# Expert products with the weights held in TensorE, and the routing weight applied at the last eviction

## What is computed

```python
router_probs = softmax(x @ gate_weight.T)              # 32 experts
router_top_value, router_indices = top_k(router_probs, 8)
...                                                    # 4 primary choices; a secondary one is moved
...                                                    # to the most similar primary if that is >= 0.5
combine = sum(one_hot(rerouted_indices) * routing_weights)     # tokens x 32
def expert_step(y, params):
    wgu, wd, cw = params                               # 384x512, 512x192, one weight per token
    g, u = split(x @ wgu.T, 2, axis=-1)
    h = silu(g) * u
    return y + h @ wd.T * cw[:, None], None
```

## Time and profile before

| | |
|---|---|
| median of 3 runs | 1722.84 us (1722.58 to 1733.0) |
| the profiled execution | 1730.1 us, of which the span from the first to the last instruction is 1728.3 us |
| mean granted TensorE clock | 0.941 of 2.4 GHz |
| busy share of the span | PE 86%, DVE 57%, ACT 41%, POOL 43% |
| PE matmuls | 11445 in the whole program |
| DMA | 269.44 MB, mean 156 GB/s |
| chain that ended last | PE 63%, DVE 15%, DMA 10%, issue 5%, ACT 4%, POOL 3% |

### The profile page before, as it was taken

One profiled execution on the slowest core, in us unless ns is written; L12 is line 12 of the kernel. 1 busy time (PEld: TensorE's weight loads), 2 busy tenths in 40 slices (PEclk: granted clock), 3 DMA queues, 4 the chain that ended last, 5 costly groups with the idle time before them and its releaser, 6 DMA issues.

```text
span 1728.3 us, 33963 instructions
## 1 busy us (share of the span) xinstructions
PE 1481.2 (86%) x11445; PEld 837.2 (48%) x11446; DVE 989.4 (57%) x1922; ACT 715.4 (41%) x1291; POOL 748.5 (43%) x671
## 2 busy tenths in 40 slices
PE   1199999986999999999998458988988999999980
PEld 0166666652444444445554314655555566565650
DVE  5767777766675757553489793433333344344437
ACT  4233433335546464643464342433333344444440
POOL 0134444443001010134345625565566766666654
PEclk9699999997999999999999568999999999999995
DMA  8211111115877676751011126999999977777868
GB/s 331 83 29 24 24 35 26 24 25 190 311 242 260 227 260 227 261 196 48 17 38 51 51 98 181 236 270 246 255 272 243 196 142 146 138 146 142 144 107 298
DMA packets 95640, 269.44 MB, mean 156 GB/s; under 512 B 15104, under 2 KB 15520, under 8 KB 90848
## 3 DMA queue, kind: packets, MB, share of 16 engines
q1 hardware_dynamic: 59968, 182.75, 31.2%
q0 software_dynamic: 35616, 85.99, 25.2%
HBM read 158.84 MB, written 101.47 MB: 151 GB/s over the span
## 4 chain that ended last, share of the span: by engine, by line
PE 63%; DVE 15%; DMA 10%; issue 5%; ACT 4%; POOL 3%; SPq 0%; DVEq 0%; ACTq 0%; POOLq 0%
PE bank L490 14%; PE bank L796 14%; PE bank L817 8%; DMA acc<-X,WA 8%; PE bank L613 6%; PE bank L619 6%; PE bank L636 6%; PE bank L787 3%; DVE ARENA L985 2%; ACT ARENA L1270 2%; PE bank L806 1%; DMA ARENA<-acc 1%; DVE ARENA L1158 1%; PE bank L717 1%; DVE bs L859 1%
## 5 line engine op out<-in xcount | busy, mean ns | idle before, releaser
L796 PE MATMUL bank<-ARENA,XT 128*128 x1908 | 368.1, 330 | 1.8 <-DVE XT L1232 1.8
L1631 POOL DMA_INDIRECT acc<-X,WA x159 | 252.7, 1589 | 185.3 <-ACT X L1270 152.4
L796 PEld LDWEIGHTS bank<-ARENA,XT 128*128 128x128 f16 x1908 | 182.0, 99 | 126.0 <-issue 11.1
L817 PE MATMUL bank<-ARENA,XT 128*128 x795 | 200.1, 383 | 26.9 <-issue 18.8
L1232 DVE COPY XT<-bank 128x1024 f16<-128x1024 f16 x159 | 109.8, 690 | 191.3 <-PE bank L787 138.0
L1270 ACT ACTIVATE ARENA<-ARENA 128x512 f16<-128x512 f32 (+1 forms) x128 | 92.7, 735 | 265.9 <-DVE ARENA L1018 131.3
L490 PE MATMUL bank<-WA,XT 128*128 128x512 f16 (+1 forms) x768 | 140.0, 337 | 69.7 <-DVE ARENA L926 34.6
L1625 POOL DMA_INDIRECT XT<-x_rows,WA x159 | 156.9, 987 | 56.8 <-issue 35.3
L1508 POOL TENSOR_TENSOR rstd<-mv,mhalf 128x1 f32<-128x1 f32 x44 | 18.9, 430 | 311.0 <-DVE mv L862 311.0
L490 PE MATMUL bank<-XT,STG 128*128 128x512 f16 x640 | 148.6, 379 | 0.0
L1242 DVE SCALAR_TENSOR_TENSOR XT<-bank,XT 128x192 f32<-128x192 f32 x159 | 66.4, 418 | 136.0 <-ACT XT L1485 114.5
(11 more groups left out here) (214 smaller groups left out, 2376.0 us busy)
## 6 DMA issues: line engine op xcount, KB each, us to landing
WA<-w_exp SPq DMA_DIRECT2D x64, 640.0 KB, 5.2
w_scratch<-WA SPq DMA_DIRECT2D x64, 640.0 KB, 3.9
ARENA<-w_scratch SPq DMA_DIRECT2D x32, 1280.0 KB
ARENA<-ARENA SPq DMA_DIRECT2D x64, 128.0 KB, 2.3
acc<-ARENA SPq DMA_DIRECT2D x18, 256.0 KB, 3.0
x_rows<-ARENA SPq DMA_DIRECT2D x17, 256.0 KB, 2.0
STG<-xT SPq DMA_DIRECT2D x8, 512.0 KB, 5.9
X<-x SPq DMA_DIRECT2D x1, 4096.0 KB, 16.3
```

The costliest lines, as they stand in the source:

```text
L796: mm = pe.matmul(d, xTb[k.u % 2][:, a * KD + kd, :], weights(sl, b, kd * 2 * DFF, 2 * DFF), start=(a, b, kd) == (0, 0, 0), stop=(a, b, kd) ...
L817: mm = pe.matmul(d, hT[k.u % 2][:, c, :], weights(sl, j, c0, DIM), start=n == 0, stop=n == 4)
L1631: pool.indirect_dma_start(acc[i % 2], bass.IndirectOffsetOnAxis(blkidx[:, i:i + 1], 0), yD[i % 4], None, compute_op=ALU.add).then_inc(y_ou ...
```

## The change

- `gate_up` holds the weights and moves the tokens. For each of three groups `c` of 128 features it makes 12 matmuls of 128 moving columns, each with its own held 128x128 of weights: 36 matmuls in place of 12. The result has features on partitions, and the host lays the 384 rows of the weights out in a new order: gate 0 to 127, then up 128 to 191 with gate 128 to 191, then up 0 to 127.
- With features on partitions h needs no transposing: `h_transposes`, `ht_evac` and `hB` go. ACT takes the SiLU in two instructions, DVE multiplies 256 columns, ACT writes the high half straight into `hT`, and DVE the low half.
- The routing weight can't be applied there any more, as tokens are now along the columns. It is the scale of `y_evac`, read from `xg` through a register, so ACT runs `load_packs` in place of DVE, and the factor 1/256 goes into the router's product (L1121).
- `expert_down` runs two blocks behind, between the first and the second group of `gate_up`. Its fifth matmul contracts over 64 rows alone, in place of the third block of `hT`.
- `gather` waits until the result of the block that used the buffer is evicted (`y_sb`).

```diff
-            def gate_up(k, sl, some):
-                d = bank[2 + k.u % 2][:, 0:2 * DFF]
-                for a, b, kd in some:
-                    mm = pe.matmul(d, xTb[k.u % 2][:, a * KD + kd, :], weights(sl, b, kd * 2 * DFF, 2 * DFF),
-                                   start=(a, b, kd) == (0, 0, 0), stop=(a, b, kd) == (1, 0, KD - 1))
+            def gate_up(k, sl, c):
+                d = bank[2 + k.u % 2][:, c * P:(c + 1) * P]
+                n = 0
+                for a, b in ((0, 0), (0, 1), (1, 0)):
+                    for kd in range(KD):
+                        mm = pe.matmul(d, weights(sl, b, kd * 2 * DFF + c * P, P), xTb[k.u % 2][:, a * KD + kd, :],
+                                       start=n == 0, stop=n == 3 * KD - 1)
+                        n += 1
                 return mm
...
-            def h_transposes(k):
...
             def expert_down(k, sl):
-                pe.wait_ge(ht_sb, k.i + 1)
+                pe.wait_ge(h_lo, k.i + 1)
                 if not k.before(2):
                     pe.wait_ge(y_sb, k.i - 1)
...
-                order = ((1, 0, base), (1, 1, base), (0, 0, base), (2, 0, base + DIM), (2, 1, base + DIM))
-                for n, (c, j, c0) in enumerate(order):
-                    mm = pe.matmul(d, hT[k.u % 2][:, c, :], weights(sl, j, c0, DIM), start=n == 0, stop=n == 4)
-                mm.then_inc(blk_done, 1)
+                pe.matmul(d, h[:, 1, :], w(0, base), start=True, stop=False)
+                pe.matmul(d, h[:, 1, :], w(1, base), start=False, stop=False)
+                pe.matmul(d, h[:, 2, :], w(0, base), start=False, stop=False)
+                pe.matmul(d, h[:, 0, :], w(0, base + DIM), start=False, stop=False)
+                pe.matmul(d, h[0:64, 0, :], w(1, base + DIM)[0:64, :], start=False, stop=True).then_inc(blk_done, 1)
...
-                if not k.before(3):
-                    expert_down(k.at(-3), expert_of(held["packs"], k.u - 3) % NSLOT)
                 sl = e % NSLOT
...
-                gate_up(k, sl, products[:8])
+                gate_up(k, sl, 0)
+                if not k.before(2):
+                    expert_down(k.at(-2), expert_of(held["packs"], k.u - 2) % NSLOT)
                 if not last:
                     gather_transposes(k.at(1))
-                gate_up(k, sl, products[8:]).then_inc(gu_ready, 1)
-                if not k.before(1):
-                    h_transposes(k.at(-1))
+                gate_up(k, sl, 1)
+                gate_up(k, sl, 2).then_inc(gu_ready, 1)
...

-                dve.scalar_tensor_tensor(h, bank[2 + k.u % 2][:, DFF:2 * DFF], cw, sgD[k.u % 2], ALU.mult, ALU.mult).then_inc(h_ready, 1)
+                if not k.before(2):
+                    dve.wait_ge(h_hi, k.i - 1)
+                dve.tensor_tensor(h.rearrange("p a n -> p (a n)"), bank[2 + k.u % 2][:, P:3 * P], sgD[k.u % 2].rearrange("p a n -> p (a n)"),
+                                  ALU.mult).then_inc(h_ready, 1)
                 dve.wait_ge(h_hi, k.i + 1)
-                dve.tensor_tensor(split[:, 0:P], h[:, 0:P], split[:, P:2 * P], ALU.subtract)
-                dve.tensor_tensor(split[:, 2 * P + 64:3 * P], h[:, P:DFF], split[:, 2 * P:2 * P + 64], ALU.subtract).then_inc(h_lo, 1)
+                dve.tensor_tensor(split[64:P, 0, :], h[0:64, 0, :], split[0:64, 0, :], ALU.subtract)
+                dve.tensor_tensor(split[:, 2, :], h[:, 1, :], split[:, 1, :], ALU.subtract).then_inc(h_lo, 1)
...

-                copy(yD[k.u % 4], bank[6 + k.u % 2][:, :], 1 / (WS * WS)).then_inc(y_sb, 1)
+                cw = xg[k.u % NG].bitcast(F32)[:, DIM:XROW][:, bass.ds(e, 1)]
+                act.activation(yD[k.u % 4], bank[6 + k.u % 2][:, :], ACT.Identity, scale=cw).then_inc(y_sb, 1)
...
-                act.activation(sgD[k.u % 2], bank[2 + k.u % 2][:, 0:DFF], ACT.Silu, scale=1 / WS).then_inc(sg_ready, 1)
-                if not k.before(1):
-                    ht_evac(k.at(-1))
+                act.activation(sg[0:64, 0, :], gu[64:P, P:2 * P], ACT.Silu, scale=1 / WS)
+                act.activation(sg[:, 1, :], gu[:, 0:P], ACT.Silu, scale=1 / WS).then_inc(sg_ready, 1)
...

             def gather(i):
                 if i >= NG:
-                    pool.wait_ge(h_ready, i - NG + 1)
+                    pool.wait_ge(y_sb, i - NG + 1)
```

More of the change, by code:

```diff
@@ L230, in build @@
         xTb = [r.take([2 * KD, P], F16) for _ in range(2)]
-        sgD = [r.take([DFF], F32) for _ in range(2)]
-        h32 = [r.take([DFF], F32) for _ in range(2)]
-        hB = [r.take([3 * P], F16) for _ in range(2)]
+        sgD = [r.take([2, P], F32) for _ in range(2)]
+        h32 = [r.take([2, P], F32) for _ in range(2)]
         hT = [r.take([3, P], F16) for _ in range(2)]
@@ L791, in weights, with expert_down @@
                 return Wslot[:, bass.ds(sl * (2 * WCOLS) + (j * WCOLS + c0), n)]
-            def gate_up(k, sl, some):
-                d = bank[2 + k.u % 2][:, 0:2 * DFF]
-                for a, b, kd in some:
-                    mm = pe.matmul(d, xTb[k.u % 2][:, a * KD + kd, :], weights(sl, b, kd * 2 * DFF, 2 * DFF),
-                                   start=(a, b, kd) == (0, 0, 0), stop=(a, b, kd) == (1, 0, KD - 1))
+            def gate_up(k, sl, c):
[6 more added lines that the diff above has]
+                        n += 1
                 return mm
-            def h_transposes(k):
+            def expert_down(k, sl):
                 pe.wait_ge(h_lo, k.i + 1)
[L802 to L809, removed]
-                pe.wait_ge(ht_sb, k.i + 1)
                 if not k.before(2):
@@ L814, in expert_down @@
                 base = KD * 2 * DFF
-                order = ((1, 0, base), (1, 1, base), (0, 0, base), (2, 0, base + DIM), (2, 1, base + DIM))
-                for n, (c, j, c0) in enumerate(order):
-                    mm = pe.matmul(d, hT[k.u % 2][:, c, :], weights(sl, j, c0, DIM), start=n == 0, stop=n == 4)
-                mm.then_inc(blk_done, 1)
-            products = [(a, b, kd) for a, b in ((0, 0), (0, 1), (1, 0)) for kd in range(KD)]
+                h = hT[k.u % 2]
+                w = lambda j, c0: weights(sl, j, c0, DIM)
+                pe.matmul(d, h[:, 1, :], w(0, base), start=True, stop=False)
[3 more added lines that the diff above has]
+                pe.matmul(d, h[0:64, 0, :], w(1, base + DIM)[0:64, :], start=False, stop=True).then_inc(blk_done, 1)
             held = {}
@@ L843, in _ @@
             every_block(pe, 8, expert_block, 8)
[L844 to L848, removed]
+            for j in (2, 1):
+                expert_down(Blk(0, NBLK - j, 8), expert_of(held["packs"], NBLK % 8 - j) % NSLOT)
         @block.vector
@@ L1223, in _ @@
             dve.scalar_tensor_tensor(blkidx, vzero, float(TOK), bank[5][:, 0:NBLK], ALU.add, ALU.add).then_inc(tables_ready, 1)
-            mine = {}
+            for u in range(2):
+                own.did(dve.memset(sgD[u][64:P, 0, :], 0.0))
+            own.settle()
             def xt_evac(k):
@@ L1467, in _, with y_evac @@
             row_hots(3, 0, ROWS_B)
[L1469 to L1475, removed]
+            theirs = {}
+            def y_evac(k, e):
                 act.wait_ge(blk_done, k.i + 2)
@@ L1478, in y_evac @@
                     act.wait_ge(y_out[k.u % 4], k.use(4) * 16)
-                copy(yD[k.u % 4], bank[6 + k.u % 2][:, :], 1 / (WS * WS)).then_inc(y_sb, 1)
+                cw = xg[k.u % NG].bitcast(F32)[:, DIM:XROW][:, bass.ds(e, 1)]
+                act.activation(yD[k.u % 4], bank[6 + k.u % 2][:, :], ACT.Identity, scale=cw).then_inc(y_sb, 1)
             def expert_block(k, fresh, last=False):
+                if fresh:
+                    theirs["packs"] = load_packs(act.engine, k)
                 act.wait_ge(gu_ready, k.i + 1)
@@ L1484, in expert_block @@
                     act.wait_ge(h_ready, k.i - 1)
[L1485 to L1487 removed]
+                sg, gu = sgD[k.u % 2], bank[2 + k.u % 2]
+                act.activation(sg[0:64, 0, :], gu[64:P, P:2 * P], ACT.Silu, scale=1 / WS)
+                act.activation(sg[:, 1, :], gu[:, 0:P], ACT.Silu, scale=1 / WS).then_inc(sg_ready, 1)
                 act.wait_ge(h_ready, k.i + 1)
                 if not k.before(2):
[L1490 to L1491 removed]
+                    act.wait_ge(blk_done, k.i)
+                copy(hT[k.u % 2][:, 0:2, :].rearrange("p a n -> p (a n)"), h32[k.u % 2].rearrange("p a n -> p (a n)")).then_inc(h_hi, 1)
                 if not k.before(2):
[L1493 to L1498 removed]
+                    y_evac(k.at(-2), expert_of(theirs["packs"], k.u - 2))
+            every_block(act, 8, expert_block, 8)
+            for j in (2, 1):
+                y_evac(Blk(0, NBLK - j, 8), expert_of(theirs["packs"], NBLK % 8 - j))
         @block.gpsimd
@@ L1666, in _layouts @@
     }
-    gu = i["L1_ffn_gate_up_proj"].transpose(0, 2, 1).reshape(EXPERTS, KD, P, 2 * DFF).transpose(0, 2, 1, 3)
+    feats = np.r_[0:P, DFF + P:2 * DFF, P:DFF, DFF:DFF + P]
```

(1 more changed line is left out.)

23 lines of the change are left out of this document (7 added, 16 removed).

## The result

The changed kernel takes 1846.9 us (median of 4 runs, 1845.8 to 1848.3), the kernel before in the same comparison 1727.3 (1722.6 to 1733.0): 119.6 us more, ratio 1.069, 95% interval 1.065 to 1.074. The profiled execution took 1846.4 us; its span is 1842.9 us against 1728.3, 114.6 more. The forecast was 1835 in a range of 1795 to 1900.

A forecast was written before the change was run, and what follows sets the result against it. PE's array mostly bounds the expert stage before; after, its sequencer's address work does: 2.4 + 2.1 - 0.1 + 0.28, unrounded 4.64 us, over 159 blocks, 738 for 627, +111 on 1722.8, said as 1835 us, range 1795 to 1900.

The forecast's parts named there:

- The address steps: PE's sequencer in gate_up: 24 weight addresses per block in place of 8, 16 more at 0.13 us, +2.1 us.
- the rival's 1710: Forecast time if PE's array, not its sequencer, set the pace at 3.53 us per block; chance 0.11.
- The sum of a block: PE's sequencer, expert stage: 2.4 base + 2.1 addresses - 0.1 dropped wait + 0.28 reload, 4.64 us per block.
- The even 4.6 us named as a sign: Expected sign in the expert stage: L1485, run once per block, would come at an even 4.6 us.
- the range's lower end: Expert stage: 1795 us, tied to 4.4 us per block; an address step of 0.10 us gave 4.2.
- The array's time: PE's matmuls and transposes per block: 3.65 + 0.05 for products - 0.17 for h's transposes, 3.53 us.
- Down products: 0: expert_down on PE: still five products of 512 columns, contracting over 64 rows changes nothing, 0 us.
- What was put at 0: ACT, DVE, POOL's gather and scatter, the router's product and the DMA-bound stretch: hidden or unchanged, 0 us.
- The router's product: L1121, four runs at 1.23 us: its form with a scalar costs 0 to +5 us, taken as 0.
- The array stays the bound: Rival, PE in the expert stage: sequencer total under 3.65 us, array 3.53 per block, 1710 us; chance 0.11.
- The load of the held operand shows: Rival, PE's products: weight loads of 0.098 us unhidden, 5.2 us per block, +200, 1923 us; chance 0.04.
- More than I count: Rival, PE: third pass recomputes addresses (2080 us), granted clock falls, or instruction fetches (from +36); chance 0.10 together.

The follow-up runs named there:

- e1: Kernel before, operands as they were, its products cut into 36 matmuls of 128 moving columns with 24 weight addresses per block; 1871.1 us, ratio 1.083.
- e2: As e1, but all three groups read the first group's weights, so 8 addresses per block; 1746.8 us, ratio 1.012.
- e12: As e10, but with each address worked out one by one, as in the change; 1832.6 us, ratio 1.061.
- e10: As e9, with TensorE's reload of the expert numbers moved behind the down products of each eighth block; 1713.2 us, ratio 0.990.
- e5: As e4, with the addresses of each group of matmuls worked out ahead of it in packed register instructions; 1772.3 us, ratio 1.026.
- e6: As e5, with the fifth down product over 128 rows in place of 64; 1763.5 us, ratio 1.019.
- e9: As e6, with the gathered block's transposes ahead of the down products and their evacuation ahead of DVE's subtractions; 1734.8 us, ratio 1.003.
- e7: Changed kernel with only the fifth down product over 128 rows in place of 64; 1846.3 us.
- e4: Changed kernel with slots read through a view of bytes, so each address is one operation and not a packed three; 1782.2 us, ratio 1.032.
- e3: Changed kernel with all three groups reading the first group's weights, so 8 addresses per block; 1786.9 us, ratio 1.034.
- e11: Kernel before with only TensorE's reload of the expert numbers moved, behind the first eight products of each eighth block; 1734.8 us, ratio 1.003.

## Why the prediction was right

**The bound.** The forecast was that the array would wait for addresses. e1 and e2, and e12 and e10, differ in the address work and in nothing else, with 124.2 and 119.4 us between them. The whole loss of 119.6 is of that size. It isn't the only layer: packing alone gives back 74.6 (e5), the other 45 lie under it and come out only with e6 (8.9), e9 (28.7) and a part of the reload's move.

**The address steps.** 24 a block, forecast and counted without exception. The 0.13 us a step, read from trains behind a reload, holds in a steady block too (7 gaps in 0.9 to 1.0 us, 15 in 2.0). The 46 ns of the rows was the trap: by it the sequencer would have fitted under the array, and the forecast would have been the rival's 1710.

**The sum of a block.** 2.4 + 2.1 - 0.1 = 4.4 us (4.36 unrounded) was forecast for a block without reload; the 118 such blocks of the loop take 4.31 on average. The reload was put at 2.2 us, 0.28 a block; it costs 2.3 in its own block and 0.2 in the one behind, 0.30 a block. What the sum put at nothing is the clock. The block behind a reload takes 4.5 us where the clock stayed at 1.00 and 5.4 where it fell to 0.50, and that is 12 x 0.87 = 10 us, 0.07 a block. Together they make 4.68, as measured (744 us over 159 blocks), where 4.64 was forecast. So the miss of some 6 us is small partly by luck: 0.05 too much for the addresses stands against 0.09 too little for reload and clock. The even 4.6 us named as a sign didn't come, as the reload's block and the one behind it stick out. And the range's lower end, 4.4 us, isn't that of the smallest step: 4.2 us would have been some 1765.

**The array's time.** 3.53 us was the sum, hidden in the changed kernel; e10 has 3.54. *Down products: 0* was wrong by 0.2 us a block (L814 and the transposes behind it), unseen at this bound (e7).

**What was put at 0.** DVE has 15% of the chain as before and ACT 3% (4%), and a steady block's chain is PE alone. DMA fell from 10% to 4%, and ACT's eviction (L1470) waited 1.2 us in the whole run, so the scatters no longer hold up the evictions. The router's product takes the same time in its new form:

```profile
L1112 DVE SCALAR_TENSOR_TENSOR WA<-WA x4: 1225/1226/1227, 870.4 to 1001.5; 128x1024 f32<-128x1024 f32 x4
```

The DMA-bound stretch keeps a share of 0.91, where under 0.9 was forecast, and a pace of 4.75 against 4.71: 2 us.

**The rivals.** *The array stays the bound*: not here, but e10 comes to it, by packed addresses and three other edits, with the sign and nearly the size that the rival gave (1710). It decides "if the sequencer's total is under 3.65", and that is what packing does. *The load of the held operand shows*: 36 pairs in 2.01 us in e10 are 56 ns each, at a granted clock of 1.00, so it doesn't. The Trainium skill (TensorE: Matmul & The Clock Gate, Back-to-back issue gap) has 81 ns for such a sustained stream; by it the 36 would take 2.9 us, and this trace disagrees. *More than I count*: the third pass uses the registers of the first (24, not 36), the granted clock did fall for parts of the stage and cost the 10 us above, which lie inside the range, and from 1100 to 1600 us the instruction queues moved 8 packets in some 13 rounds, no more than a trickle:

```profile
q8 instruction: 3, 0.05, 0.0%
q14 instruction: 5, 0.04, 0.0%
```

## What to carry to other kernels

Count the distinct run-time addresses of an inner loop, not only its matmuls, and price them by the distance between their starts; the duration that a row shows was a third of the price here. A change that cuts matmuls into more pieces with addresses of their own spends the sequencer's slack first and then its whole cost. And when a bound is lifted, read the chain again: behind the addresses stood an evacuation in the wrong place of DVE's queue, behind it a reload, and only with these taken off too did the change become worth having (1713 against 1730).

## What the runs showed of the hardware that was not expected

- A register instruction of TensorE's sequencer costs 0.124 us in a train, if it packs three operations, and 0.112 if it is a single one (e4). Packing 28 a block into 7 took 74.6 us off (e5); an instruction with several additions is followed by the next after 0.14 to 0.17 us there. So the count of instructions costs far more than that of operations.
- A matmul over 64 rows among such over 128 costs 0.1 us, and the transposes behind it another 0.1 (L814 and L786 above; gone in e10's chain, L822 and L788).
- The sequencer's lead isn't a fixed time. The same reload exposes 1.0 us more behind products of 128 columns than behind those of 384 (e2). In these traces it is a number of matmuls: from the first register instruction of a reload 17 of them start before the array stands still, in the kernel before, e2, e3, e5, e9 and e10 alike, the last one after 1.6, 0.9, 0.9, 0.9, 0.9 and 1.6 us. Where address steps come just before the reload it is less: 7 in the changed kernel and in e11, 4 or 5 in e1. No run varied it by itself.
- The lower clock behind a reload came after gaps of some 2.1 us in the changed kernel, but not after each of them; in e10, with gaps of 0.43 and 1.15 us, it didn't come at all between 1060 and 1660 us.
